# Latent attention: the causal mask is added by TensorE in the scores' banks, and the copy of the scores goes

## The reference, cut to what matters

```
Q = (xr @ Wq)  16 heads of 16;   K, V = (xr @ Wk), (xr @ Wv)  4 groups, repeated to 16 heads
scores = Q K^T / sqrt(16)                      # per head, 64 x 64
mask   = triu(-1e9, k=1)
attn   = softmax(scores + mask)
out    = attn V, heads joined, @ Wo
h = x + out
```

## Time and profile before

| | |
|---|---|
| median of 3 runs | 1037.44 us (1036.21 to 1040.33) |
| time of the profiled execution | 1034.94 us |
| its span | 1033.1 us |
| PE, PEld busy | 786.5, 571.0 us (76%, 55%) |
| DVE, ACT, POOL busy | 519.6, 440.8, 437.2 us (50%, 43%, 42%) |
| granted PE clock in 40 slices of 25.8 us, in tenths | 9999999889879888999996756886556999999995 |

### The profile page before, as it was taken

How to read it: one execution, slowest core, us unless ns; L and a number is a source line. 1 busy time by engine, 2 the same in 40 slices (tenths; PEclk the granted TensorE clock), 3 DMA queues, 4 the chain that set the end, 5 groups by cost and what they waited for, 6 DMA issues and landing times.

```text
span 1033.1 us, 21352 instructions
## 1 busy us (share of the span) xinstructions
PE 786.5 (76%) x7200; PEld 571.0 (55%) x7200; DVE 519.6 (50%) x1397; ACT 440.8 (43%) x1523; POOL 437.2 (42%) x637
## 2 busy tenths in 40 slices
PE   2788987699779566999975626765555999999980
PEld 1676766588644235777754415654432566666660
DVE  3466766467733344667665765666231333223323
ACT  1667667246514225777751023766102333333320
POOL 4566654434468768687722334354341000000005
PEclk9999999889879888999996756886556999999995
DMA  8322214723331545454410003122292065152004
GB/s 285 137 67 79 70 53 143 240 73 95 123 124 54 190 133 170 147 172 136 155 51 0 0 0 122 43 83 97 92 391 77 27 223 179 49 189 93 16 23 122
DMA packets 66199, 116.83 MB, mean 113 GB/s; under 512 B 6576, under 2 KB 22704, under 8 KB 65456
## 3 DMA queue, kind: packets, MB, share of 16 engines
q1 hardware_dynamic: 57936, 105.25, 30.3%
q10 hardware_dynamic: 6624, 6.03, 1.8%
q0 software_dynamic: 1536, 4.20, 1.3%
HBM read 81.11 MB, written 34.34 MB: 112 GB/s over the span
## 4 chain that ended last, share of the span: by engine, by line
PE 48%; DVE 15%; POOL 13%; ACT 9%; issue 8%; DMA 4%; ACTq 0%; SPq 0%; DVEq 0%; POOLq 0%; another core or an unknown queue 0%
ACT probs L1208 6%; PE ps L622 4%; PE ps L1046 4%; PE ps L1047 4%; PE ps L1048 4%; PE ps L638 3%; PE ps L1069 2%; PE ps L1071 2%; PE ps L1070 2%; PE ps L1058 2%; PE ps L520 2%; DVE probs L1710 2%; POOL probs L1454 2%; PE ps L662 2%; PE ps L521 2%
## 5 line engine op out<-in xcount | busy, mean ns | idle before, releaser
L1393 POOL TENSOR_TENSOR piece_out<-piece_in,piece_out 128x512 f16<-128x512 f32 x96 | 116.6, 1215 | 7.7
L1609 POOL DMA_INDIRECT pt<-y_rows,neg x16 | 15.4, 960 | 233.4 <-DMA y_rows<-vbuf 228.8
L2133 DVE TENSOR_TENSOR probs<-ps,ctx_t 128x512 f32<-128x512 f32 x46 | 29.6, 686 | 154.0 <-PE ps L1048 154.0
L622 PE MATMUL ps<-pack_const,probs 128*128 128x128 f32 x512 | 74.3, 278 | 17.0 <-issue 13.1
L1358 POOL TENSOR_TENSOR var<-mv,half 128x1 f32<-128x1 f32 x48 | 9.6, 199 | 179.4 <-DVE mv L1625 107.7
L622 PEld LDWEIGHTS ps<-pack_const,probs 128*128 128x128 f32 x512 | 55.9, 140 | 37.7 <-issue 26.0
L1392 POOL CAST piece_out<-piece_in 128x512 f16<-128x512 f32 x96 | 62.2, 648 | 23.0 <-DMA piece_in<-in_w 22.1
L1046 PE MATMUL ps<-arena,qbuf 128*128 x184 | 70.7, 384 | 0.0
L1047 PE MATMUL ps<-arena,qbuf 128*128 x184 | 70.5, 383 | 0.0
L1048 PE MATMUL ps<-arena,qbuf 128*128 x184 | 70.3, 382 | 0.0
L1158 ACT ACTIVATE probs<-ps,mx 128x256 f32<-128x256 f32 x128 | 59.2, 487 | 15.6 <-DVE mx L1721 15.6
(11 more groups left out here) (285 smaller groups left out, 2178.5 us busy)
## 6 DMA issues: line engine op xcount, KB each, us to landing
piece_in<-in_w SPq DMA_DIRECT2D x96, 256.0 KB, 2.8
w_parts<-piece_out SPq DMA_DIRECT2D x96, 256.0 KB, 2.1
arena<-w_parts SPq DMA_DIRECT2D x8, 3072.0 KB, 12.7
ctx_t<-in_ctx SPq DMA_DIRECT2D x32, 256.0 KB, 2.8
x_rows<-piece_out SPq DMA_DIRECT2D x1, 2944.0 KB, 17.3
qbuf<-x_rows ACTq DMA_DIRECT2D x23, 128.0 KB, 2.4
y_rows<-vbuf ACTq DMA_DIRECT2D x23, 128.0 KB, 1.9
arena<-in_xa SPq DMA_DIRECT2D x2, 1282.0 KB, 7.8
```

Source lines behind the costliest of these rows:

```text
L622: last = pe.transpose(AB[:, o:o + P], pr[:, 2 * c + n, kt * P:(kt + 1) * P], ident)
L1393: pool.tensor_tensor(both[:, PIECE:], src, both[:, 0:PIECE], ALU.subtract).then_inc(piece_split, 1)
```

## The change

- PE, `score`: in "la", before it waits for the copied queries and keys, four multiplications write the mask into columns 0 to 255 of the four banks: identity (stationary) by the mask, broadcast over four heads (moving, 256 columns), with start set. The 16 score multiplications then accumulate on it (start not set).
- DVE, `row_maxima`: the four mask additions and the signal "shifted" go. "la" takes the maxima from S, as "sa" does.
- ACT, `exps`: the exponentials of "la" read S and write `probs`, as in "sa".
- PE, `values`: it waits for "exped" of the tile before in both stages.

```diff
--- before.py
+++ after.py
@@ -323,7 +323,7 @@
                                        "rstd normed")),
             "rope": signals(each(TILES, "squared rstd roped turned xt")),
             "blocks": signals({"summed": BLOCKS}),
-            "la": signals({**inner_counts, **each(TILES, "shifted squared summed_up row_hi row_lo")}),
+            "la": signals({**inner_counts, **each(TILES, "squared summed_up row_hi row_lo")}),
         }
 
         loads = {"x": ["x"], "x_rest": ["x_rest"], "const": ["const"], "xa0": ["xa0"], "sa": ["sa"], "ffn": ["ffn"], "ssm": ["four", "ssm"],
@@ -749,13 +749,18 @@
                         last.then_inc(g["r_projected"].sem, 1)
 
                 def values(i):
-                    hold(pe, g["exped" if st == "sa" else "shifted"], i)
+                    hold(pe, g["exped"], i)
                     for c in range(DC):
                         last = pe.matmul(S[:, 256:512], tile_of_x(i, c), wv[:, c, :], start=c == 0, stop=c == DC - 1)
                     last.then_inc(g["v_projected"].sem, 1)
 
                 def score(i):
 
+                    if st == "la":
+                        for j in range(4):
+                            pe.matmul(S[:, j * 512:j * 512 + 256], ident,
+                                      W["const"]["causal"].unsqueeze(1).broadcast_to([P, 4, SEQ]),
+                                      start=True, stop=False, skip_group_check=True)
                     hold(pe, g["qk_copied"], i + 1)
                     for f in range(2):
                         for b in range(2):
@@ -764,8 +769,8 @@
                             for j in range(4):
                                 r = slice(32 * j, 32 * j + 32)
                                 o = j * 512 + f * P + b * SEQ
-                                last = pe.matmul(S[:, o:o + SEQ], q[r, :], kk[r, :], start=st == "la" or f + b == 0,
-                                                 stop=st == "la", skip_group_check=st == "sa")
+                                last = pe.matmul(S[:, o:o + SEQ], q[r, :], kk[r, :], start=st == "sa" and f + b == 0,
+                                                 stop=st == "la", skip_group_check=True)
                     if st == "sa":
                         hold(pe, g["r_taken"], i + 1)
                         for f in range(2):
@@ -1205,7 +1210,7 @@
                     for n in heads:
                         p = probs[:, s * 2048 + n * SEQ:s * 2048 + (n + 1) * SEQ]
                         o = (n // 4) * 512 + (n % 4) * SEQ
-                        last = act.activation(p, p if st == "la" else S[:, o:o + SEQ], ACT.Exp, scale=scale,
+                        last = act.activation(p, S[:, o:o + SEQ], ACT.Exp, scale=scale,
                                               bias=mx[:, s * HEADS + n:s * HEADS + n + 1],
                                               accum_out=ssum[:, s * HEADS + n:s * HEADS + n + 1])
                     if n == HEADS - 1:
@@ -1811,22 +1816,8 @@
                     hold(dve, g["scored"], i + 1)
                     src = S.rearrange("p (j o) -> p j o", j=4)[:, :, 0:256]
                     m = mx[:, s * HEADS:(s + 1) * HEADS]
-                    if st == "la":
-                        p = probs[:, s * 2048:s * 2048 + 1024]
-                        for j in range(4):
-                            last = dve.tensor_tensor(p[:, j * 256:(j + 1) * 256].rearrange("p (n k) -> p n k", k=SEQ),
-                                                     src[:, j, :].rearrange("p (n k) -> p n k", k=SEQ),
-                                                     K["causal"].unsqueeze(1).broadcast_to([P, 4, SEQ]), ALU.add)
-                            if j < 3:
-                                chain.mark(last)
-                        last.then_inc(g["shifted"].sem, 1)
-                        hold(dve, g["shifted"], i + 1)
-                        chain.join()
-                        chain.link(dve.tensor_reduce(m, p.rearrange("p (n k) -> p n k", k=SEQ), AX.X, ALU.max, negate=True))
-                    else:
-                        chain.link(dve.tensor_reduce(m.rearrange("p (j n) -> p j n", j=4),
-                                                     src.rearrange("p j (n k) -> p j n k", k=SEQ), AX.X, ALU.max,
-                                                     negate=True))
+                    chain.link(dve.tensor_reduce(m.rearrange("p (j n) -> p j n", j=4),
+                                                 src.rearrange("p j (n k) -> p j n k", k=SEQ), AX.X, ALU.max, negate=True))
                     dve.tensor_scalar(m, m, scale, None, ALU.mult).then_inc(g["maxima"].sem, 1)
 
                 def scale_probs(i, s):
```

## The result

| | before | after |
|---|---|---|
| median, us (13 runs each) | 1036.19 (1034.24 to 1040.33) | 1042.06 (1039.8 to 1044.77) |
| profiled execution, own time / span, us | 1034.94 / 1033.1 | 1043.18 / 1041.3 |
| stage "la" in the profile, us | 121.25 | 126.12 |
| granted clock over the span | 0.871 | 0.879 |

The changed kernel takes 1.0056 of the time before, 95% interval [1.0043, 1.007], 5.9 us more. Of the 8.2 us between the two spans, 4.87 stand there, 2.8 ahead of it and 0.5 behind. So I read the stage, not the span.

A forecast was written before the change was run, and what follows sets the result against it. In "la" the DVE-ACT-POOL chain binds before, a loop through PE after. Full-clock sum -0.8, first step's clock loss +2.0, six steps at +1.0: +7.2 us on a median of 1037.44, 1044.6 us, range 1034 to 1053.

The forecast's parts named there:

- my marks: In "la", starts of DVE's value copy (L1806), one per tile; forecast 11.3 us apart at full clock, 12.5 or more at half.
- The second loop: In "la", last exponential, values, mask, scores, turn, copies, exponentials become the bound: 11.34 us a step against 12.01 before.
- Step one of the argument: In "la", values wait for the last exponential instead of "shifted", putting PE on the path; called the larger part.
- The mask's price: Eight passes on PE per tile, directly behind the values: 1.72 us at full clock, up to 2.3; 3.4 to 4.1 at half.
- Exponentials and maxima from the banks: In "la", 16 exponentials reading PSUM take 4.84 us instead of 5.42; maxima from PSUM booked as no change.
- The full-clock sum: Whole stage at 2.4 GHz: 1.72 + 0.66 + 0.67 + 0.2 - 2.7 - 1.4 = -0.8 us.
- The clock: PE dry 2.8 us before the values brings half clock onto the path: +2.0 us first step, +1.0 in each of six.
- A: Rival: the clock holds in "la" because PE is busier; 1038.6 us, range 1036 to 1041; chance 25%.
- B: Rival: PE at half clock over the whole path in nearly each step of "la", +4.3 a step; 1059.7 us; chance 9%.
- C: Rival: DVE-POOL loop stays the bound, 10.38 us a step, if the mask takes 0.8 us; 1029.5 us; chance 8%.

The follow-up runs named there:

- experiments 1: Kernel before, with only the values' wait in "la" changed to the last exponential; mask additions and score copy stay: 1045.71 us, ratio 1.0087 to the kernel before.
- experiment 8: Kernel before with the later wait of the values alone, plus five dead multiplications on PE behind each tile's mixing: 1040.70 us, ratio 1.0055 to the kernel before.
- experiment 4: Changed kernel with the values projected a step earlier, so only mask and scores wait for the last exponential: 1028.27 us, ratio 0.9928 to the kernel before.
- experiment 3: Changed kernel with five dead multiplications of the mask's shape on PE behind each tile's mixing in "la": 1035.75 us, ratio 0.9989 to the kernel before.
- experiment 5: Changed kernel with the mask and identity in f16, four single passes instead of eight: 1030.27 us, ratio 0.9939 to the kernel before.
- experiment 2: Changed kernel without the four mask multiplications, so causality is left out of "la": 1035.27 us, ratio 0.9988 to the kernel before.
- experiment 10: Changed kernel with values earlier, f16 mask, four dead multiplications a tile, and POOL's low half moved ahead of root and sum: 1022.55 us, ratio 0.988 to the kernel before.

## Why the prediction was right

Forecast 1044.6, measured 1042.06; by the profiled execution 1042.1 and 1043.18. The stage carries most of it: +4.87 measured. By my marks the stage was to grow by 7.2. The mechanism came as forecast; the number is nearer than its terms deserve, as the last but one point says.

- **The second loop.** Right. The values start 0.04 us after the last exponential, and the chain is values, mask, scores, turned rows, copies, exponentials. Step one of the argument (the wait, more than the mask, changes the bound) is shown by experiments 1 and 8. That the wait alone costs 9 us, more than the whole change, I had not worked out: the removed additions and the cheaper exponentials then bring 4.1 us of stage back, though the mask has been added.
- **The mask's price.** Predicted 1.72, measured 1.73 in the chain where the full clock holds; the two others are 1.99 behind idle time (experiment 4) and 3.14 at the half clock.
- **Exponentials and maxima from the banks.** Predicted 4.84 and no change; measured 4.86 (2.48 and 2.38 in the chain of one step) and 1214 ns. The busy time says the opposite for ACT, since the mean of one exponential in "la" rises from 333 to 361 ns, yet 16 of them end 0.56 us earlier. Groups of the stage alone:

```profile
L1819 DVE TENSOR_REDUCE mx<-ps 128x16 f32<-128x1024 f32 x8 | 9.7, 1214 | 0.0
L1213 ACT ACTIVATE probs<-ps,mx 128x64 f32<-128x64 f32 x128 | 38.5, 361 | 9.6 <-DVE mx L1821 9.6
```

- **The full-clock sum.** Predicted -0.8 us, measured 4.87 - 6.6 = -1.7. Step two was 10.75 (predicted 10.78), step three 11.15 in experiment 3 (11.19), the steady ones 11.15 to 11.17 where I had 11.34: four of those are 0.7 us, most of the difference. It went in ACT's terms: the copies of the probabilities took 0.97 in the chain and not 1.09, and the 16 exponentials of a steady step 4.72 (0.63, 1.71, 2.38) and not 4.84. By the value copies the first mark came 1.54 later (predicted 1.72) and the part behind the last was 1.36 shorter (1.4). The marks were to be 11.3 us apart at the full clock and 12.5 or more at the half: 11.15 and 12.81.
- **The clock.** Predicted 2.0 in the first step and 1.0 in each of six, 8.0. Measured against the same steps of experiment 3 or the untouched ones beside them: 1.68 in the first (12.43 against 10.75) and 1.67, 1.65 and 1.64 in steps three, four and six (12.82, 12.81 and 12.81 against 11.15), 6.6 in all. Against experiment 3 the part behind the last maxima lost more, but that part is not dearer than before: there PE was at the half clock already. The size of one fall is the upper end of the 1.2 to 1.7 that I gave for one; the mean of 1.0 hid that a step loses either 1.65 or nothing. Half of the six were hit, in this one profile. I had the place of a fall wrong: I put it at up to 0.8 us ahead of the values, or just behind their start, since in the kernel before it came 2.0 to 2.9 us after PE ran dry. Here it came 3.6 to 5.2 us after, 0.3 to 1.4 behind the start of the values, so none of it was spent in the idle time.
- **What offsets what.** The two terms were each mis-sized, -0.8 for -1.7 and 8.0 for 6.6, and both came out lower, so the errors add up: 7.2 forecast, 4.9 measured in the stage. Two things outside the terms blur this, and that is luck. In the medians the difference was 5.9 us, 1.0 of it not in the stage, where I had forecast nothing; and the forecast of 1044.6 stands on a median before of 1037.44, which with more runs is 1036.19. The miss of 2.5 us is 1.3 of the change and 1.25 of that. In the profiled execution 3.4 of the 8.2 us stand outside the stage, which is why 1042.1 comes so near 1043.18.
- **The rivals.** A (the clock holds) is refuted by the windows; experiment 3 makes it true from the second step on and gives 1035.75, beside the 1038.6 that I had for it, in which I had booked no gain from the full clock behind the last mark. B didn't come: no low stretch between 646.3 and 724.6 us of the changed kernel outlasted 3.3 us. C was excluded by the mask's price, and experiment 5, which meets its condition, gives its step, 10.29 for 10.38. Its time of 1030.27 is near 1029.5, but as a ratio to the kernel before it is 0.9939 where C had 0.9924. The condition is not enough by itself: experiment 2, with no mask at all, met it and ran at 11.0 to 11.2 a step, since the half clock fell on PE's work.

The Trainium skill (TensorE: Matmul & The Clock Gate, "HAM oscillation") was cited for bursts that start at the low clock. The measurement agrees only in part: with 2.8 us of idle time in each steady step, three of the six bursts behind the first step met the low clock and the others ran at the full one. Which steps are hit is open. The length of the gap doesn't decide it: in the changed kernel steps with 2.76 us were hit and spared, and in experiment 5 none of five with 2.6 to 3.0 us was hit. The DMA share doesn't either: it was 0.34 to 0.52 in the three later falls and 0.00 in the first.

## What to carry to other kernels

Before moving work onto an engine that the chain doesn't touch, look at what its new wait lets run: here the wait for the last exponential cost 9 us, the mask's passes 1.7 a tile, and the removed additions only 1.34 a tile. Cost what a resource hides at both clocks, for 2.2 us of TensorE work under a cover of 2.9 become 4.0. When idle time brings the half clock onto the path, moving work out from behind the wait (experiment 4) or making it short (experiment 5) gave more here than filling the gap, and a filler must be no longer than the gap: the eight dead passes of experiment 10 became the bound.

## What the runs showed of the hardware

- Dead multiplications sped a kernel up: +40 calls of 256 columns, -6.3 us (1042.06 to 1035.75), with the granted clock at 1.00 for the whole of 646.30 to 724.60.
- In experiment 3 the filler left 0.4 to 0.6 us of idle time ahead of the values and no fall came; in experiment 8 falls came in the three steps with 2.3 to 2.4 us left and not in the three with 0.7 to 1.4; in experiment 5, with 2.6 to 3.0 us in each of five steps, none did.
- The four low stretches at the values of the changed kernel's "la" are 3.3 us long each, and each cost the path 1.64 to 1.68 us, half its length.
- The granted clock fell 3.6 to 5.2 us after PE ran dry in the changed kernel, when PE was at work again, and 2.0 to 2.9 us after in the kernel before.
- A 128x256 multiplication in f16 runs in one pass where the f32 one takes two: four calls 0.60 us against 1.73.
